# Graph attention layer: who makes the low parts and diagonals of the first chunk, GpSimd or VectorE

## What is computed

```
Wh = x @ W[h];  f1, f2 = Wh @ a1[h], Wh @ a2[h]
e  = leaky(f1[:, None] + f2[None, :]); e = where(adj > 0, e, -1e9)
h  = elu(softmax(e) @ Wh), the four heads side by side (2048 wide)
o  = elu(the same with one head, W_out (2048 x 512), a_out)
y  = relu(o @ w1 + b1) @ w2 + b2 + o
out = norm(x + norm(y) * gamma + beta)
```

## Time and profile before

| | |
|---|---|
| median of 3 runs | 2168.59 us (2168.57 to 2170.19) |
| the profiled execution | 2170.8 us, span 2169.0 us |
| TensorE, weight loads | 2125.0 us (98%), 1923.6 us (89%) |
| VectorE | 1590.4 us (73%) |
| ScalarE, GpSimd | 949.7 us (44%), 958.3 us (44%) |
| first matmul of chunk 0's gather | 48.45 us after the start of the span |

### The profile page before, as it was taken

The page is one execution under the profiler, slowest core; times in us unless marked ns, Lnnn a source line. Parts: engine busy times, 40 slices in busy tenths (PEclk is TensorE's granted clock), DMA queues, the critical chain, the costliest instruction groups (busy, mean ns, idle before and its releaser), DMA issues.

```text
span 2169.0 us, 42902 instructions
## 1 busy us (share of the span) xinstructions
PE 2125.0 (98%) x13860; PEld 1923.6 (89%) x13860; DVE 1590.4 (73%) x3202; ACT 949.7 (44%) x2186; POOL 958.3 (44%) x1015
## 2 busy tenths in 40 slices
PE   5999999999999999999999999999999999999997
PEld 2899999999999999999999999999999988999997
DVE  3867776677777767677677777777777669999998
ACT  2544444444444444444444444444444443434443
POOL 3633333333333333333333333333333337777776
PEclk7999999999999999999999999999999999999999
DMA  8011111111111111111111111111111133333342
GB/s 287 30 40 40 39 39 39 39 39 39 39 39 39 39 39 39 39 39 39 39 40 42 40 39 39 39 39 39 39 39 40 44 108 128 134 126 135 121 140 87
DMA packets 73861, 134.04 MB, mean 62 GB/s; under 512 B 8672, under 2 KB 8800, under 8 KB 73824
## 3 DMA queue, kind: packets, MB, share of 16 engines
q1 hardware_dynamic: 73824, 133.57, 18.4%
HBM read 99.98 MB, written 33.55 MB: 62 GB/s over the span
## 4 chain that ended last, share of the span: by engine, by line
PE 93%; POOL 1%; issue 1%; DVE 1%; ACT 0%; DMA 0%; POOLq 0%; DVEq 0%; SPq 0%; ACTq 0%
PE h_ps L415 11%; PE h_ps L417 11%; PE h_ps L416 11%; PE t_ps L431 11%; PE t_ps L430 11%; PE t_ps L429 11%; PE h_ps L509 3%; PE h_ps L511 2%; PE h_ps L510 2%; PE t_ps L525 2%; PE t_ps L523 2%; PE x_ps L364 2%; PE t_ps L524 2%; PE x_ps L399 1%; PE x_ps L400 1%; PE h_ps L400 1%
## 5 line engine op out<-in xcount | busy, mean ns | idle before, releaser
L1075 POOL TENSOR_TENSOR h_lo<-h_full,h_hi 128x256 fp32r<-128x256 f32 x512 | 391.8, 765 | 1045.5 <-ACT h_hi L672 1036.1
L415 PE MATMUL h_ps<-g_hi,wh_hi 128*128 128x256 f32 x2048 | 587.4, 287 | 1.8 <-DVE h_full L893 1.3
L417 PE MATMUL h_ps<-g_hi,wh_lo 128*128 128x256 f32 x2048 | 578.9, 283 | 0.0
L416 PE MATMUL h_ps<-g_lo,wh_hi 128*128 128x256 f32 x2048 | 578.1, 282 | 0.0
L891 DVE TENSOR_SCALAR h_full<-h_full 128x256 f32<-128x256 f32 x512 | 281.6, 550 | 359.0 <-ACT h_full L643 357.8
L431 PE MATMUL t_ps<-wo_hi,h_lo 128*128 128x512 f32 x1024 | 403.6, 394 | 0.0
L430 PE MATMUL t_ps<-wo_lo,h_hi 128*128 128x512 f32 x1024 | 403.2, 394 | 0.0
L429 PE MATMUL t_ps<-wo_hi,h_hi 128*128 128x512 f32 x1024 | 401.9, 393 | 0.0
L415 PEld LDWEIGHTS h_ps<-g_hi,wh_hi 128*128 128x128 f32 x2048 | 386.7, 189 | 16.9 <-DVE h_full L893 2.4
L416 PEld LDWEIGHTS h_ps<-g_lo,wh_hi 128*128 128x128 f32 x2048 | 385.7, 188 | 13.3
L417 PEld LDWEIGHTS h_ps<-g_hi,wh_lo 128*128 128x128 f32 x2048 | 386.1, 189 | 0.0
(11 more groups left out here) (122 smaller groups left out, 3837.2 us busy)
## 6 DMA issues: line engine op xcount, KB each, us to landing
x_dup<-in_x SPq DMA_DIRECT2D x248, 128.0 KB, 2.6
attn<-in_x_t SPq DMA_DIRECT2D x64, 256.0 KB, 2.8
mid<-o_buf SPq DMA_DIRECT2D x64, 256.0 KB, 2.0
o_in<-mid SPq DMA_DIRECT2D x32, 512.0 KB, 3.6
x_again<-in_x SPq DMA_DIRECT2D x32, 512.0 KB, 4.3
out<-res SPq DMA_DIRECT2D x64, 256.0 KB, 2.0
wt_raw<-in_w_heads_t SPq DMA_DIRECT2D x4, 1024.0 KB, 9.5
wh_raw<-in_w_heads SPq DMA_DIRECT2D x4, 1024.0 KB, 17.0
```

The costliest lines, as they stand in the source:

```text
L415: mm(to, w_hi, g_hi[:, h, ft, :], start=ft == 0, stop=False)
L416: mm(to, w_hi, g_lo[:, h, ft, :], start=False, stop=False)
L417: last = mm(to, w_lo, g_hi[:, h, ft, :], start=False, stop=ft == FT - 1)
L1075: tt(h_lo[:, v % RING, :], h_full[:, v % 2, :], h_hi[:, v % RING, :].bitcast(F32), ALU.subtract).then_inc(h_lo_done, 1)
```

## The change

Ahead of the loop, GpSimd makes x's low part, then the first 4 low weights, waits for `attn_done` and makes the other 12, so none is left in the loop. VectorE makes the two diagonals of chunk 0. ScalarE rounds 12 pieces of the heads' weights ahead of `exps(0)` and 4 behind it, none in the loop.

```diff
--- before.py
+++ after.py
@@ ScalarE, the tile loop @@
                     if first:
-                        if v < FT:
-                            head_round(3 * FT + v)
                         wo_round(v)
@@ ScalarE, ahead of the loop @@
-            for i in range(2 * FT):
+            for i in range(3 * FT):
                 head_round(i)
             exps(0)
-            for i in range(2 * FT, 3 * FT):
+            for i in range(3 * FT, HEAD_TILES):
                 head_round(i)
@@ VectorE, ahead of the loop @@
             logits_out(0)
-            for b in range(CB):
-                dve.wait_ge(x_hi_done, b + 1)
-                rest = x_split[N:P, b, :]
-                tt(rest, x_first[N:P, b, :], rest.bitcast(F32), ALU.subtract).then_inc(x_lo_done, 1)
+            dve.wait_ge(logits_sb, 1)
+            for k, part in enumerate((f2_hi, f2_lo)):
+                tt(diag[:, k, :, :, :], part.unsqueeze(3).to_broadcast([P, CP, NH, N]),
+                   node_ident[:, :].unsqueeze(1).unsqueeze(1).to_broadcast([P, CP, NH, N]), ALU.mult)\
+                    .then_inc(diag_done, 1)
             scores(0)
@@ GpSimd, the tile loop @@
-                    if first and v < 2 * FT:
-                        head_rest(2 * FT + v)
...
                             pool.wait_ge(h_lo_done, c * TILES + v + 1)
-                            if first:
-                                pool.wait_ge(wh_lo_done, min(2 * FT + v + 1, HEAD_TILES))
                             x_rest(c + 1, v // 3)
@@ GpSimd, ahead of the loop @@
             pool.wait_ge(const_done, 1)
-            diagonal(0)
-            for i in range(2 * FT):
+            for b in range(CB):
+                pool.wait_ge(x_hi_done, b + 1)
+                rest = x_split[N:P, b, :]
+                tt(rest, x_first[N:P, b, :], rest.bitcast(F32), ALU.subtract).then_inc(x_lo_done, 1)
+            pool.wait_ge(x_lo_done, CB)
+            for i in range(FT):
+                head_rest(i)
+            pool.wait_ge(attn_done, 1)
+            for i in range(FT, HEAD_TILES):
                 head_rest(i)
             chunks(pool, iteration)
```

## The result

The change makes the kernel faster by a small but clear amount: 2164.73 us (2163.0 to 2165.83) against 2169.4 us (2168.33 to 2170.57), 12 executions each. The ratio is 0.9977, with a 95% interval of 0.9968 to 0.9986: 5.0 us of 2169.4, between 3.0 and 6.9 (the two medians lie 4.7 apart). The forecast was 3.3 us and 2165.3.

A forecast was written before the change was run, and what follows sets the result against it. TensorE, busy 98% of the span, was taken as the bound, so only closing its gaps gains. Front 0.5 plus loop 2.8 gave 3.3 us: from the median 2168.59 to 2165.3 us, range 2162.6 to 2167.6.

The forecast's parts named there:

- The side of noise: Whole kernel: 0.2%, 4.3 us, taken as about what can be measured; chances same 0.64, faster 0.33, slower 0.03.
- The rule of holds: VectorE's two-input SBUF and small instructions wait for the end of GpSimd's running one; a GpSimd one behind is held 0.45 us.
- the forecast chain: First stretch: first low weight holds the cast, second the subtraction, third and fourth the diagonals; spread at 35.53, leaky free.
- The front: Softmax of chunk 0, up to the gather: transposes at 42.73 instead of 43.21, gather at 48.0; gain 0.5 us.
- rival 1: First stretch: VectorE's cast passes ahead of the first low weight; gain 4.4 to 5.4 us, 2163.2 to 2164.2; chance 0.28.
- The loop: Chunk 0's tile loop: no low weights left for GpSimd, TensorE's gaps shrink; gain 2.8 us, bounds 1.2 and 3.2.
- the 0.3 to 0.4 us held back for waits that would stay: Loop: 0.3 of the second spread's 2.21 us wait stays, and 0.9 of the other 1.0 us goes.
- The signs of being wrong: Changed profile: the cast isn't held, the diagonals cost VectorE over 1 us, or TensorE's waits on h_full grow.
- Costs put at nothing: ScalarE's extra rounds end before exps; GpSimd's twelve low weights end at 57.5, ahead of h_lo due at 58.6.
- 2 (the loop stays bound by VectorE): Loop: VectorE's pile in tiles 5 to 8 replaces GpSimd; only 0.5 to 1.5 us gained in all; chance 0.13.
- 3 (ScalarE behind the weights): First stretch: exps wait in ScalarE's queue for the third head's weights; slower if landing is from 41.5 on; chance 0.05.
- the 2.9 us: Sum instead of 3.3 us if VectorE holds the ports its whole instruction: the two diagonals 0.2 us later each.

The follow-up runs named there:

- e5: Change with GpSimd's work ahead of the loop laid around VectorE's two-input instructions by waits for diagonals, scores and attn_done; 2163.17 us, ratio 0.9964.
- e7: Change with no low weight ahead of attn_done, all 16 behind it; 2165.37 us, ratio 0.9983 to before.
- e4: The change itself again, no edit, for a second profile of its front; 2163.84 us, ratio 0.9975 to before.
- e11: Repeat of e5, GpSimd's work laid around VectorE's two-input instructions; 2163.31 us, ratio 0.9972 to before.
- e12: The change itself once more, no edit, for a third profile of its front; 2163.98 us, ratio 0.9976 to before.
- e1: Kernel before with only the loop relieved: all 16 low weights ahead of it, ScalarE's order of the change; 2164.91 us against 2169.38, ratio 0.9981.
- e8: e1 with four of the eight low weights put back in the loop, at tiles 4 to 7; 2166.99 us, ratio 0.9987 to before.
- e6: Change with one more wait: GpSimd begins the first four low weights only behind the two diagonals; 2162.74 us, ratio 0.9965 to before.
- e10: Repeat of e6, the first four low weights behind the two diagonals; 2163.08 us, ratio 0.9972 to before.
- e3: Change with chunk 0's two diagonals back on GpSimd, between x's low part and the four low weights; 2165.5 us, ratio 0.9984 to before.
- e9: e5 with the last two low weights of the heads on VectorE, in its idle times; 2161.05 us, ratio 0.9961 to before.
- e2: Change with only the front: loop of GpSimd and ScalarE as before, 4 low weights behind attn_done; 2167.64 us against 2169.38, ratio 0.9994.

## Why the prediction held, point by point

**Right in kind and place.** Gains in the two stretches named: of the profiles' 7.1 us, 6.7 are there at the end of the loop marks (135.01 against 128.31). The measured 5.0 us lie in the range, 1.7 above the forecast. That the forecast time, 2165.3, came within 0.6 us of the measured 2164.73 is partly luck: it started from a median of 2168.59 out of three runs, and from the 2169.4 of twelve it would have been 2166.1. The side of noise that was held likelier was the wrong one: 0.64 for under 0.2%, and 0.23% was measured (the interval 0.14 to 0.32% holds the bound).

**The rule of holds: right for the front, not for all.** It was worked out from a few instructions, and it gave the front of e5 to 0.1 us (15 expected, 14.98) and that of e7 at the end of its range (14.5 to 15.5, 14.46). e4 shows the forecast chain step by step. But that a held instruction waits for the end of the *running* one of GpSimd isn't always so: in e11 one waited for three. It is the only such one in the fourteen profiles, and why it wasn't let through sooner is open.

**The front: 0.5 us forecast, 1.0 to 1.4 measured.** The sum took the cast just behind the first low weight, the worst point of the tooth: a hold lasts until the running instruction ends, so whoever comes just behind its start pays it all. In e4, with the same order, the cast came 0.55 us behind it, and copy to gather was 18.14 instead of the forecast 48.0 less 29.36 = 18.6: the half microsecond is that. In the other two the holds paid were fewer, as in rival 1, seen in 2 of 3 profiles where its chance was 0.28, though what held the cast or the subtraction was x's fourth low part. Its gains of 1.6 and 2.6 were too high, since `leaky`, and in e12 `masked`, were then held. That the order varies was seen; that the start of GpSimd's row (23.69 to 26.40) and the copy (27.53 to 29.73) move by 2 to 3 us each between executions was not.

**The loop: 2.8 us forecast, 3.8 measured (e1, after).** This is the term that was mis-sized. Two parts: the 0.3 to 0.4 us held back for waits that would stay weren't needed in the profile of the change (e4 still has 0.2), and the gaps were counted by the listed idle time, 3.20 us. From start to start of the matmuls they were 2.38, 0.42 and 0.89 us beyond the usual step, 3.7 in all: the modelled tail of a matmul (0.39 us listed where the step is 0.23) covers 0.16 us of each gap. That the first four weights caused the big gap is shown by e8.

**The signs of being wrong.** By the letter two of the three came true: in e12 the cast isn't held (0.18 us), and in the change's profile the diagonals take VectorE 1.65 and 1.75 us. The first is the order of rival 1; the second is holds, since in e5, e6, e10 and e11 both take 0.69 on VectorE, as the sum had it. TensorE's waits on `h_full` are gone.

**Costs put at nothing: right.** ScalarE's 12 roundings ended at 34.03, and exponentials started at 38.35; GpSimd's last low weight ended at 55.6, 1.1 us ahead of its `h_lo`. That second cover is thin: e5 (57.04) and e7 (59.48) show the cost when it is gone.

**Rivals.** 2 (the loop stays bound by VectorE) fell: no wait in 54 to 90 us. 3 (ScalarE behind the weights) fell: the third head was there at 31.84. The Trainium skill (SBUF — State Buffer, Who interferes with whom) calls the ports that both engines share an exclusive lock, and says where it speaks of VectorE's two-port modes that whoever issues first gets them for the whole instruction. Taken so for VectorE's two-input instructions as well, as the prediction does, it isn't what the runs show: four low weights alone take 4.96 us (a third of the 14.88 for twelve), 5.38 in e4 with one diagonal in between and 5.87 in the change's profile with two, so a diagonal of 0.69 us holds 0.42 to 0.49. Nor does the 2.9 us that the prediction gives by that reading come out of its own chain: only the second diagonal stands behind a low weight that VectorE has held, so 0.2 us are to be taken off once, which leaves 3.1.

**The 7.1 us of the profiles.** 1.1 of them are the start: the logits' 16 matmuls took 2.97 us before, at a granted clock of 0.50 from 28 us on, and 1.95 after, at 1.00. Nothing was changed ahead of them, and e4, the same kernel as after, took 3.11, so this is no gain of the change; 0.4 more lies between the gather and the restart of the head (8.21 and 7.82 us), 7.37 in e4. Executions of one kernel differ by 2 to 3 us in time, and these two stretches, where the granted clock changes between 1.0 and 0.5 at a point that differs from one execution to the next, show such differences. That they make up all of the spread was not tested.

What stays open: what let e11's elu stand for three low weights, and how often that happens; how much of the front is due to the diagonals on VectorE as such (e3's x was late), and whether e6, e5 and the change differ at all by their medians. e9 is 2.9 us ahead of the change by medians on one chip, from 5 and 10 executions; its interval to before (0.9948 to 0.9975) overlaps that of the change by 0.0008.

## What to carry to other kernels

Where VectorE's instructions with two inputs in SBUF, or its casts and `tensor_scalar`s from SBUF to SBUF, run beside GpSimd's, however small, count each as waiting for the end of the running one at least, and lay GpSimd's work into VectorE's waits for other engines, with semaphores, rather than one behind the other; then check what GpSimd's later end does, since here 1.4 us of lateness in e5 gave back about half of what the front won. Reductions aren't concerned: `highest` took 0.69 us or less in all 32 chunks before, the first beside running low weights. Take gaps of TensorE from start to start, not from listed idle time. And where two chains of different origin meet, take the phase of one profile as one case of several: here three profiles gave three orders.

## What was not expected of the hardware

The granted clock fell to 0.50 behind a wait of 2.2 us in e2 and, in e11, behind 16 small matmuls (1.85 us) and a wait of 1.69 us, but not behind 2.21 us in the loop of before. A short wait can thus cost twice: in e2 the loop (53.83 to 132.47) took 78.64 us against 78.35 before, though its later waits were smaller. A cast of 8 columns took up to 1.26 us beside GpSimd, 0.17 alone. An elu instruction of 128x256 stood through three low weights, 3.83 us (e11). And two low weights on VectorE beside a running GpSimd took 0.68 and 0.69 us: at 39.03 it began ahead of GpSimd's (39.20), and at 44.39 GpSimd's was all but over (it ended at 44.51). GpSimd's low weights beside them took 1.65 and 1.76 us instead of 1.26.
